# Weights of the output stage loaded where their low halves will lie, z alone in the raw slots

## The reference

```python
x = x + attn(layernorm(x))     # x: 4 batches of 512 tokens, HID = 512, fp32
x = x + ffn(layernorm(x))

# attn: H = 32 heads in 8 groups, D = 128, chunks of C = 128 tokens
q, k = rope(x @ Wq.T), rope(x @ Wk.T);  v = x @ Wv.T
dt = softplus(x @ Win.T + dt_bias);  G = cumsum(dt * -exp(A_log_bias))   # within a chunk
y  = (q k^T * exp(G_i - G_j), causal) @ (v*dt)  +  (q * exp(G)) @ state_before
state = state * exp(G_last) + (k * exp(G_last - G))^T @ (v*dt)
z  = rmsnorm(y) * gnorm_w * silu(x @ Wg.T)
out = z.reshape(L, H*D) @ Wo.T
# ffn: dense W, b, and E = 8 experts of rank 16, weighted by a softmax over q.k
```

## Time and profile before

| | |
|---|---|
| median of 3 runs | 1835.56 us (1832.38 to 1835.94) |
| the profiled execution's own time | 1833.96 us |
| its span in the profile | 1832.2 us |
| mean granted clock of PE | 0.994 |
| PE busy | 1791.7 us (98%) |
| DVE, ACT, POOL busy | 1242.5 us (68%), 665.8 us (36%), 709.9 us (39%) |
| attention's last step on PE | about 1303.8 to 1340.6 us |

### The profile page before, as it was taken

The page is one execution under the profiler, slowest core; times in us unless marked ns, Lnnn a source line. Parts: engine busy times, 40 slices in busy tenths (PEclk is TensorE's granted clock), DMA queues, the critical chain, the costliest instruction groups (busy, mean ns, idle before and its releaser), DMA issues.

```text
span 1832.2 us, 27509 instructions
## 1 busy us (share of the span) xinstructions
PE 1791.7 (98%) x8728; PEld 1457.4 (80%) x8728; DVE 1242.5 (68%) x2321; ACT 665.8 (36%) x2151; POOL 709.9 (39%) x757
## 2 busy tenths in 40 slices
PE   7998999999999999999999999999979999999998
PEld 5787888888888888888888888888757888888886
DVE  5235888888888888888888888888864333333332
ACT  3432444344344444443434434443543121112121
POOL 2223555455545555555545554655401101010101
PEclk9999999999999999999999999999989999999999
DMA  5233333423323322333332333322564232222321
GB/s 185 87 104 94 108 95 101 116 86 111 116 84 107 121 87 80 114 110 92 98 116 86 111 114 87 109 90 85 173 210 138 77 99 78 95 88 84 96 77 46
DMA packets 145952, 190.30 MB, mean 104 GB/s; under 512 B 9104, under 2 KB 79760, under 8 KB 145808
## 3 DMA queue, kind: packets, MB, share of 16 engines
q1 hardware_dynamic: 145808, 188.58, 34.0%
HBM read 141.89 MB, written 46.66 MB: 103 GB/s over the span
## 4 chain that ended last, share of the span: by engine, by line
PE 86%; DMA 2%; DVE 1%; ACT 1%; issue 0%; SPq 0%; POOL 0%; ACTq 0%; DVEq 0%; POOLq 0%
PE p_proj L85 28%; PE p_kept L85 14%; PE p_tok L1337 9%; PE p_kept L1337 8%; PE p_y L798 6%; PE p_score L85 5%; PE p_y L797 5%; PE p_cst L783 4%; PE p_qa L85 3%; PE p_f L1520 2%; DMA w_raw<-z_scratch 1%; PE p_f L1531 1%; PE p_tok L766 1%; DMA w_raw<-in_wo_t 0%; DMA out_dram<-q 0%
## 5 line engine op out<-in xcount | busy, mean ns | idle before, releaser
L85 PE MATMUL p_proj<-shared,wq_hi 128*128 128x512 f32 x744 | 273.6, 429 | 0.0
L114 POOL TENSOR_TENSOR q<-rope_a,rope_b 128x512 f32<-128x512 f32 x128 | 164.9, 1288 | 267.7 <-DVE rope_b L106 267.7
L1064 ACT ACTIVATE square<-p_y 128x128 f32<-128x128 f32 x512 | 134.5, 278 | 263.7 <-PE p_y L798 261.7
L798 PE MATMUL p_y<-v_tok,probs 128*128 128x128 f32 x1024 | 182.1, 275 | 0.0
L85 PE MATMUL p_proj<-wg_hi,shared 128*128 128x512 f32 x528 | 178.2, 418 | 0.0
L85 PE MATMUL p_kept<-wg_hi,shared 128*128 128x512 f32 x560 | 176.6, 396 | 0.0
L85 PEld LDWEIGHTS p_proj<-shared,wq_hi 128*128 128x128 f32 x744 | 139.8, 188 | 45.3 <-issue 14.8
L939 DVE SCALAR_TENSOR_TENSOR z<-p_y,srstd,gate 128x128 f32<-128x128 f32 x512 | 143.7, 343 | 37.5 <-issue 24.5
L1039 ACT ACTIVATE probs<-g_row,stab 128x128 f32<-128x128 f32 x512 | 164.3, 409 | 9.2 <-POOL g_row L1153 9.2
L1752 POOL TENSOR_TENSOR var<-mv,eps 128x1 f32<-128x1 f32 x16 | 3.0, 190 | 418.2 <-DVE mv L1602 418.2
L1171 POOL TENSOR_TENSOR srstd<-svar,mhalf 128x4 f32<-128x4 f32 x128 | 157.4, 1230 | 10.0
(11 more groups left out here) (225 smaller groups left out, 4211.5 us busy)
## 6 DMA issues: line engine op xcount, KB each, us to landing
g_row<-g_scratch SPq DMA_DIRECT2D x128, 256.0 KB, 4.3
z_scratch<-z_st SPq DMA_DIRECT2D x256, 128.0 KB
w_raw<-z_scratch SPq DMA_DIRECT2D x62, 512.0 KB, 6.6
e_row<-e_scratch SPq DMA_DIRECT2D x96, 256.0 KB, 4.0
w_raw<-in_wq_t SPq DMA_DIRECT2D x16, 512.0 KB, 7.2
w_raw<-in_wg_t SPq DMA_DIRECT2D x16, 512.0 KB, 6.0
v_tok<-v_scratch SPq DMA_DIRECT2D x32, 256.0 KB, 2.9
w_raw<-in_wo_t SPq DMA_DIRECT2D x12, 512.0 KB, 5.4
```

The lines of the kernel that those rows point to most:

```text
L85: mm = pe.matmul(out, lhs[a], rhs[e], start=(i == 0 and j == 0), stop=(i == len(pairs) - 1 and j == 2))
L114: pool.tensor_tensor(out, keep["rope_a"][:, s, :], keep["rope_b"][:, s, :], ALU.add).then_inc(keep["roped"], 1)
L798: mm = pe.matmul(p_y[c % 2][:, h, :], probs[:, c % 2, h, :], v_tok[:, b % 2, c, :], start=(c == 0), stop=True)
L1064: s = act.activation(square[:, h, :], p_y[c % 2][:, h, :], ACT.Square, scale=2.0 / float(np.sqrt(D)), accum_out=ssum[:, c, h:h + 1])
```

## The change

Wo, wqa and ws are no longer loaded into raw slots. Each piece is loaded into the place of its own low part, through an fp32 tile that lies on the same bytes (`twice`); ACT makes the high part from there, and DVE writes the low part over the raw value. The pieces have semaphores of their own, one for two pieces (`weights_in`), and ACT waits for both. z alone uses the four raw slots, in the order q = 2j + s. Four rows of Wo's second half (`wo_early`, heads 16 to 19) take the place of the tables `tab`, `cos`, `sin`, `rope_a` and `rope_b`, which the last step does not need. The order of the list, the places of the loads and the heads done in the last step change:

```diff
             def step(g, b, n):
                 if not ahead(n):
+                    load_last_weights(n)
                     sp.wait_ge(y_done, NC * n)
-                    for k in (3, 4, 5):
-                        load_opening(sp, io, keep, k)
+                    load_first_z(sp, keep, 1, 1)
+                    sp.wait_ge(roped, ROPED * (n + 1))
+                    sp.wait_ge(stab_set, n + 1)
+                    for a in (8, 9):
+                        load_weights(sp, io, keep, WO, a)
...
-                    if not ahead(n):
-                        for k in ((6,), (7, 8), (9,), ())[c]:
-                            load_opening(sp, io, keep, k)
-                    if before_last(n) and c == 2:
+                    if not ahead(n) and c == 2:
+                        load_first_z(sp, keep, 0, 2)
+                        load_first_z(sp, keep, 1, 2)
+                    if before_last(n, 2) and c == 2:
+                        load_last_weights(n)
+                    if before_last(n, 1) and c == 1:
+                        load_last_weights(n)
+                    if before_last(n, 1) and c == 2:
...
-                        for k in range(3):
-                            load_opening(sp, io, keep, k)
+                        for s, j in ((0, 0), (1, 0), (0, 1)):
+                            load_first_z(sp, keep, s, j)
...
+            def load_last_weights(n):
+                sp.wait_ge(gate_set, NC * n)
+                for a in range(2):
+                    load_weights(sp, io, keep, WO, 2 * (n - 1 - (LAST - B + 1)) + a)
...
             steps(sp, first, step)
             store_z(KVH - 1, B - 1, LAST, 1)
-            for k in range(10, LOADED_EARLY):
-                load_opening(sp, io, keep, k)
+            load_last_weights(LAST + 1)
...
-                        first_heads(n, 0, range(2 * c, 2 * c + 2))
+                        first_heads(n, 0, 0, (range(0, 3), range(3, 5), range(5, HP))[c])
                     mix(g, b, n, c)
-                first_heads(n, 0, range(6, HP))
-                first_heads(n, 1, range(HP))
+                first_heads(n, 1, 0, range(HP))
+                first_heads(n, 0, 1, range(ATTENTION_HEADS))
...
-                    for k in ((2,), (3, 4), (5,), (6,))[c]:
+                    for k in ((3,), (4, 5), (6,), (7,))[c]:
                         opening_low(dve, keep, k)
...
                 if before_last(n):
-                    for k in range(2):
+                    for k in range(3):
                         opening_low(dve, keep, k)
...
-OPENING = [(Z, 0, 0), (WO, 0), (WO, 1), (Z, 1, 0), (WO, 2), (WO, 3), (WO, 4), (WO, 5),
-           (WO, 6), (WO, 7), (Z, 0, 1), (WO, 8), (Z, 1, 1), (WO, 9),
...
-SPLIT_EARLY = 8
+EARLY = 4
+OPENING = [(WO, 0), (WO, 1), (Z, 0, 0), (WO, 2), (WO, 3), (Z, 1, 0), (WO, 4), (Z, 0, 1), (WO, 5),
+           (WO, 6), (WO, 7), (Z, 1, 1), (WO, 8), (WO, 9), (Z, 0, 2), (WO, 10), (WO, 11), (Z, 1, 2),
+           (WO, 12), (WO, 13), (Z, 0, 3), (WO, 14), (WO, 15), (Z, 1, 3)] + [(w, kt) for w in (WQA, WS) for kt in range(KT)]
+SPLIT_EARLY = 9
+ATTENTION_HEADS = 4
...
+def load_first_z(sp, keep, s, j):
+    q = 2 * j + s
+    if q >= SLOTS:
+        sp.wait_ge(keep["lo_set"], OPENING.index((Z, q % 2, (q - SLOTS) // 2)) + 1)
+    load_z_piece(sp, keep, s, j, q % SLOTS)
+def load_weights(sp, io, keep, kind, a):
+    into = weights_part(keep, kind, a, 1, "raw_")
...
+    sp.dma_start(into, piece).then_inc(keep["weights_in"][kind, a // 2], 16)
...
+def twice(nc, stack, name, shape):
+    with nc.sbuf_tensor(f"raw_{name}", shape, F32) as raw:
+        pass
+    return raw, stack.enter_context(nc.sbuf_tensor(name, shape, F32R))
...
 def opening_high(act, keep, k):
-    act.wait_ge(keep["raw_in"][k % SLOTS], 16 * (k // SLOTS + 1))
     kind, a = OPENING[k][:2]
     if kind == Z:
+        q = 2 * OPENING[k][2] + a
+        act.wait_ge(keep["raw_in"][q % SLOTS], 16 * (q // SLOTS + 1))
+        wait_ge(act, keep["heads_done"], q - 1)
+        split_high(act, keep, a, q % SLOTS)
...
+        act.wait_ge(keep["weights_in"][kind, a // 2], 16 * 2)
...
             def first():
                 load_x(0, 0)
-                for k in range(LOADED_EARLY, len(OPENING)):
-                    load_opening(sp, io, keep, k)
+                for a in range(10, 14):
+                    load_weights(sp, io, keep, WO, a)
+                load_first_z(sp, keep, 0, 3)
+                for a in range(14, NW):
+                    load_weights(sp, io, keep, WO, a)
                 for s in range(2):
                     sp.wait_ge(z_out[s], 16 * TB * B * KVH)
-                sp.wait_ge(lo_set, len(OPENING) - KT)
+                for kt in range(KT):
+                    load_weights(sp, io, keep, WQA, kt)
+                load_first_z(sp, keep, 1, 3)
+                for kt in range(KT):
+                    load_weights(sp, io, keep, WS, kt)
+                sp.wait_ge(lo_set, OPENING.index((Z, 1, NP - 1)) + 1)
...
                     if isinstance(i, int) and i == 2 and j < ZSLOTS:
-                        sp.wait_ge(lo_set, len(OPENING) - SLOTS + j + 1)
+                        sp.wait_ge(lo_set, OPENING.index((Z, j, NP - 2)) + 1)
```

More of the change, by code:

```diff
@@ L598, in steps, with before_last @@
             group(KVH - 1)
-        def before_last(n):
-            return isinstance(n, int) and n == LAST - 1
+        def before_last(n, by=1):
+            return isinstance(n, int) and n == LAST - by
         def has_last(n):
@@ L809, in straight, with first_heads @@
                 last_step(KVH - 1, B - 1, LAST)
-            def first_heads(n, s, some):
+            def first_heads(n, s, j, some):
                 if s == 0:
@@ L816, in first_heads @@
                     taken(n - 1, GATE_UNIT[3])
-                heads(pe, keep, (p_tok, p_proj[2])[s][:, :, :].rearrange("p h t -> p (h t)"), s, 0, s, opening=True, some=some)
+                heads(pe, keep, (p_tok, p_proj[2])[s][:, :, :].rearrange("p h t -> p (h t)"), s, j, s, opening=True, some=some)
             def last_step(g, b, n):
@@ L1235 @@
 Z, WO, WS, WQA = "z", "wo", "ws", "wqa"
-OPENING = [(Z, 0, 0), (WO, 0), (WO, 1), (Z, 1, 0), (WO, 2), (WO, 3), (WO, 4), (WO, 5),
-           (WO, 6), (WO, 7), (Z, 0, 1), (WO, 8), (Z, 1, 1), (WO, 9),
-           (WO, 10), (WO, 11), (Z, 0, 2), (WO, 12), (Z, 1, 2), (WO, 13),
-           (WO, 14), (WO, 15), (Z, 0, 3), (Z, 1, 3)] + [(w, kt) for w in (WQA, WS) for kt in range(KT)]
-SPLIT_EARLY = 8
-LOADED_EARLY = SPLIT_EARLY + SLOTS
-assert len(OPENING) % SLOTS == 0 and WH * (SPLIT_EARLY - 2) <= (B - 1) * KT
+EARLY = 4
[4 more added lines that the diff above has]
+ATTENTION_HEADS = 4
 def number(i, j):
@@ L1252, in load_z_piece, with weights_part, wo_part @@
         "a s p h t -> p (a s) (h t)")).then_inc(keep["raw_in"][slot], 16)
[L1255 to L1265, removed]
-    else:
[L1267 to L1274, removed]
+def load_first_z(sp, keep, s, j):
[5 more added lines that the diff above has]
+    into = weights_part(keep, kind, a, 1, "raw_")
+    if kind == WO:
+        piece = io["wo_t"][a * WH * P:(a + 1) * WH * P, :].rearrange("(h p) n -> p h n", p=P)
+    else:
+        piece = io["w_t" if kind == WS else "wqa_t"][a * P:(a + 1) * P, :]
+    sp.dma_start(into, piece).then_inc(keep["weights_in"][kind, a // 2], 16)
+def weights_part(keep, kind, a, e, as_=""):
+    return wo_part(keep, e, a * WH, WH, as_) if kind == WO else keep[as_ + kind][:, a, e, :]
+def wo_part(keep, e, h, n, as_=""):
+    if h < H // 2:
+        return keep[as_ + "shared"][:, h:h + n, e, :]
+    h -= H // 2
+    return keep[as_ + "wo_early"][:, h:h + n, e, :] if h < EARLY else keep[as_ + "wo_rest"][:, h - EARLY:h - EARLY + n, e, :]
+def twice(nc, stack, name, shape):
+    with nc.sbuf_tensor(f"raw_{name}", shape, F32) as raw:
+        pass
+    return raw, stack.enter_context(nc.sbuf_tensor(name, shape, F32R))
 def by_half(tile):
@@ L1295, in opening_high @@
 def opening_high(act, keep, k):
-    act.wait_ge(keep["raw_in"][k % SLOTS], 16 * (k // SLOTS + 1))
     kind, a = OPENING[k][:2]
     if kind == Z:
[L1300 to L1305, removed]
-    else:
-        act.activation(wo_part(keep, 0, a * WH, WH), keep["raw"][k % SLOTS].rearrange("p (h n) -> p h n", h=WH), ACT.Copy,
-                       scale=keep["gn"][:, 0:1]).then_inc(keep["hi_set"], 1)
+        q = 2 * OPENING[k][2] + a
+        act.wait_ge(keep["raw_in"][q % SLOTS], 16 * (q // SLOTS + 1))
+        wait_ge(act, keep["heads_done"], q - 1)
+        split_high(act, keep, a, q % SLOTS)
+    else:
+        act.wait_ge(keep["weights_in"][kind, a // 2], 16 * 2)
+        hi, raw = weights_part(keep, kind, a, 0), weights_part(keep, kind, a, 1, "raw_")
+        if kind == WO:
+            act.activation(hi, raw, ACT.Copy, scale=keep["gn"][:, 0:1]).then_inc(keep["hi_set"], 1)
+        else:
+            act.activation(hi, raw, ACT.Copy).then_inc(keep["hi_set"], 1)
 def opening_low(dve, keep, k):
@@ L1315, in opening_low @@
     if kind == Z:
```

(32 more changed lines are left out.)

## The result

The changed kernel takes 1810.57 us (median of 4 runs, 1809.74 to 1811.59), the kernel before 1835.68 us beside it: ratio 0.9867, 95% interval 0.9853 to 0.9882. That is 25 us less where 2.4 were forecast, and outside the stated range.

The account below looks back on a forecast made before the run. PE was taken as busy nearly throughout, except at the seam between the last attention step and the output stage. Terms 1.1 − 0.4 + 0.8 + 0.85 = 2.35 gave 1835.56 − 2.4 = 1833.2 us, range 1829 to 1837.5.

Parts of the forecast that it names:

- Everything else the change could shorten is already hidden: Whole kernel: beyond PE's listed waits, 10.6 us for `wq_lo` and four of about 1 us, nothing can be gained.
- The long gap: Seam before the output stage: pieces 6 and 7 land late, but four heads move ahead; 2.75 − 1.6 = 1.1 us gained.
- the 5 us at half clock, with no gain or loss: Just behind the seam's wait: PE's lowered clock stays as before, since the gap is still about 10 us.
- The rival of a fast landing: Seam: pieces 6 and 7 land after 3.9 us, a gain of 7.6 us, 1828.0 us; chance 0.12.
- the gap eat it all: Seam: pieces 6 and 7 land after 11 us or more, no change, 1835.1 us; chance 0.22.
- The last step: Last attention step: earlier DVE start against a g row queued behind five loads; ends 0.4 us later, bounds −0.8 and +3.
- s: How much later the last attention step ends: +0.4 us taken, bounds −0.8 and +3.
- the rival of slower: Last attention step: g row lands at 1318.1 or later and delays the stores; 5.4 us more, 1838.6 us; chance 0.10.
- After the gap: Output stage: earlier loads of wqa and z(2,0) shorten PE's waits for `xn` by 0.8 us and `hwn` by 0.85 us.
- The sum: Whole kernel: 1.1 − 0.4 + 0.8 + 0.85 = 2.35, about 2.4 us less.

Follow-up runs that it names:

- Experiment 1: Kernel before with only `gn` allocated ahead of `shared`, which moves `shared` by 32 bytes: 1811.99 us beside 1833.23, ratio 0.989.
- experiment 2: Changed kernel with `gn` allocated behind `shared` again, so `shared` is back in its old place: 1829.64 us beside 1833.23, ratio 0.9982.
- experiment 10: Changed kernel with Wo pieces 6 and 7 loaded ahead of the last `store_z` instead of behind it: 1801.09 us beside 1833.53, ratio 0.9825.
- experiment 3: Changed kernel with 32 bytes of padding ahead of `shared`, all matmul tiles of attention and output at 0 mod 64: 1811.32 us beside 1833.23.
- experiment 8: Changed kernel with 32 bytes of padding ahead of `wg` alone: 1820.2 us beside 1833.39, ratio 0.9924.
- experiment 11: Changed kernel with pieces 6 and 7 loaded ahead of the last `store_z` and `n_wv` at the offset of `shared`: 1799.87 us beside 1833.39, ratio 0.9816.
- experiment 9: Changed kernel with 32 bytes of padding ahead of `n_wv`, so it starts at 32 mod 64 like `shared`: 1808.88 us beside 1833.53, ratio 0.9866.
- experiment 6: Changed kernel with `shared` read through a view 16 bytes into its tile, 16 bytes apart from wq, wk, wg, z: 1829.05 us beside 1833.53.

## Why the prediction was wrong

**The step that failed** is the sentence "Everything else the change could shorten is already hidden", and with it the costing of the change itself: it went through loads, splits and waits, and nowhere through the places of the tiles, though the diff moves `shared` and `gn` in the allocation. I took the duration of a matmul as given. In its place: `shared` started 32 bytes off wq, wk, wg and z mod 256, and the move of `gn` ahead of it made them equal. Experiment 1 has this alone at 1811.99 beside 1833.23 (21 us), experiment 2 the rest of the change alone at 3.6 us by its median and 3.3 by its ratio. By the medians the two are 24.8 us of the 25.1 measured, by the ratios 23.5 of 24.4.

The count agrees: 288 units (9 in each of 31 steps, 4 in the last, 5 in the norm stage) of some 0.06 us are 17 us, and 32 lots of eight heads with Wo in `shared` (two in each of 16 tiles), 5.60 to 5.45 us, are 4.8 us: 22 us. The values of the norm stage cancel: the half with `wg` got faster, the half with `n_wv` slower.

**None of the rivals had it**: all four argued about the seam. What could have told: the kernel before contains both speeds. `p_kept<-wo_rest` and `p_kept<-shared` are the same matmul of the same shape on the same engine, at 5.45 and 5.60 us for 24, and I copied the first number without asking why the second was larger; so are 389 ns for `n_wv_hi` and 396 for the rest of `shared`.

Point by point, the rest of the working held:
- **The long gap**: landing 9.06 us (9.1), wait 10.9 us (about 10), the lower clock again. To keep "the 5 us at half clock, with no gain or loss" was no safe term, though: the last section shows how much it scatters. The rival of a fast landing fell: 9.06 and 9.18 us. The fit of the Trainium skill (DMA: Bandwidth & Descriptors, Anatomy of one DMA), from which 3.2 us for 512 KB is an estimate, is given there for DMAs issued from GpSimd; these loads are issued by SP, behind four stores, and it does not hold for them. Nor did the gap eat it all: 11 us were not reached.
- **The last step**: from its start to the first of the last stores 34.5 us before (1303.70 to 1338.21), 34.7 in experiment 2 (1302.03 to 1336.71): s = +0.2 for +0.4. The g row was as late as estimated and cost no more than that, so the rival of slower fell too.
- **After the gap**: the waits for `xn` and `hwn` went, 0.8 and 0.85 us.
- **The sum** for this part, 2.4 us, stands against 3.3 (1.7 to 5.1) in experiment 2. Its profile has 3.5 us in the last step and the seam, of which 1.0 is a cheaper restart: 24 matmuls behind the wait took 8.22 us before, 2.6 more than the 5.60 of the full clock, and 12 took 4.45 in experiment 2, 1.65 more than 2.80. That lies within the scatter of this price (last section) and is not the change's. Without it 2.5 us are left for the 2.4 forecast; with terms of a few tenths each, so close a match is in part luck.

The seam was thus sized rightly and was a seventh of the result.

## What to carry to other kernels

When a diff changes the order, the size or the number of tiles, write down where every matmul operand starts before and after, and compare the two operands of each pair mod 256; here it decided 2 to 3% of every fp32r matmul of 512 columns whose pair was concerned, far from the edit. Look for one and the same matmul form with two durations in one trace: it is a price that can be had back without touching an instruction. And a load that waits only for a buffer belongs ahead of a batch of stores in its queue, not behind it (experiment 10).

## What the runs showed of the hardware that was not expected

- **Offset of the operands.** fp32r matmuls of 512 columns with a new stationary operand each take 227 ns start to start (2.72 us for 12) when both operands start at the same offset mod 256, and mostly 229 to 235 ns (2.75 to 2.82 us for 12) when they are 32, 64 or 128 bytes apart. The price depends on which of the two is where: at 16 apart it is nearly nothing with `shared` stationary and the highest, 2.82 us, with `shared` moving. Both at 128 (`n_wv`, before), at 160 (after) or at 192 (experiment 3) was equally fast. Why is not shown. It was seen with starts rounded to 32 bytes and once 16 apart, and in fp32r with 512 columns alone; the fp32 matmuls of 128 columns in experiment 8 did not show it.
- **The units that stay at 2.77 us.** In the kernels with equal offsets about one unit in four is at 2.77 us in place of 2.72 (after, 706.30). No run looked for its cause.
- **The clock after a gap scatters.** After a wait of 2.8 us with the clock at 1.00 throughout, the next 5 us were at 0.67 on average in experiment 10 and at 1.00 in experiment 11, with the same loads and the same wait. After 10.9 us of waiting (the kernel after) the clock was already low during the wait and low for a shorter while behind it than in the kernel before:

```profile
1325.30:1336.10 10.80, 0.00 (x0) 0.00 (x0) 1.25 (x2) 2.43 (x3) 0.00 (x0) 0.67 0.98 297
1336.10:1341.10 5.00, 4.91 (x15) 3.95 (x16) 4.76 (x5) 3.22 (x4) 0.00 (x0) 0.70 1.05 354
```

The first 12 matmuls behind waits of 10.7 to 11.3 us took between 4.36 us (experiment 9) and 5.49 (experiments 3 and 6), against 2.72 to 2.82 at the full clock. In experiment 10 they took 4.59, so there the shorter gap did not save the price of the slow matmuls; in experiment 11 it did. One execution of each is profiled, and what decides between them is not shown. A single restart is therefore good to 1 us only, and a difference of that size at a seam is no sign of an edit.
